# About 40 steps of a hand-ordered two-layer attention and expert kernel take other places in their engines' order

## The reference

```
x = x + attn1(ln(x))        # scores against 1601 memory tokens of the sequence, / 16, masked, softmax, readout
x = x + experts(ln(x))      # 8 experts (width 256), top 2 of the router: sum of w * (silu(h Wg) * (h Wu)) Wd
x = x + attn3(ln(x))        # q = h Wq; scores against the same 1601 tokens; only the 54 largest of a row stay; softmax; readout; Wo
x = x + ffn4(x)             # inputs rounded to 8 bits, weights to -1, 0, 1; w1 (256 to 1024), exact gelu, rounding, w2 (1024 to 256)
```

## Time and profile before

| | us |
|---|---|
| median of three runs | 501.22 |
| runs | 501.73, 499.03, 501.22 |
| the profiled execution | 500.69 |
| its span | 498.6 |
| outside the span | 2.1 |

### The profile page before, as it was taken

How to read it: one execution, slowest core, us unless ns; L and a number is a source line. 1 busy time by engine, 2 the same in 40 slices (tenths; PEclk the granted TensorE clock), 3 DMA queues, 4 the chain that set the end, 5 groups by cost and what they waited for, 6 DMA issues and landing times. The chain is left out here.

```text
span 498.6 us, 7119 instructions
## 1 busy us (share of the span) xinstructions
PE 418.6 (84%) x2445; PEld 342.0 (69%) x2452; DVE 381.3 (76%) x833; ACT 181.2 (36%) x264; POOL 92.5 (19%) x72
## 2 busy tenths in 40 slices
...
GB/s 248 350 238 216 157 140 227 133 97 163 175 132 107 149 170 128 136 176 139 169 189 78 152 140 116 176 143 152 102 23 11 133 5 128 0 111 3 11 0 11
DMA packets 60330, 63.96 MB, mean 128 GB/s; under 512 B 3964, under 2 KB 60040, under 8 KB 60296
## 3 DMA queue, kind: packets, MB, share of 16 engines
...
## 5 line engine op out<-in xcount | busy, mean ns | idle before, releaser
L482 POOL TENSOR_TENSOR gu_lo<-gu_stage,gu_hi 128x1024 fp32r<-128x1024 f32 x32 | 76.1, 2383 | 153.5 <-ACT gu_hi L547 153.5
L783 PE MATMUL O<-wd_ring,hid 128*128 128x256 f32 x256 | 62.8, 381 | 4.7 <-DVE x_res L968 4.5
L538 ACT ACTIVATE pT<-T 128x512 f32<-128x512 f32 x64 | 31.6, 513 | 80.0 <-PE T L721 69.4
L1017 DVE MAX8 cand_h<-fold 128x8 f32<-128x801 f32 x56 | 55.2, 985 | 0.3
L783 PEld LDWEIGHTS O<-wd_ring,hid 128*128 128x128 f32 x256 | 45.5, 189 | 12.4 <-DVE x_res L968 6.4
L739 PE MATMUL O<-pT,v_ring 128*128 128x128 f32 (+1 forms) x416 | 52.6, 287 | 0.3 <-ACT pT L538 0.3
L707 PE MATMUL S<-k_ring,xT 128*128 128x400 f32 (+2 forms) x128 | 49.4, 533 | 3.6 <-DVE mx1c L896 2.8
L739 PEld LDWEIGHTS O<-pT,v_ring 128*128 128x128 f32 (+1 forms) x416 | 51.1, 203 | 1.4 <-issue 1.1
L735 PE MATMUL O<-v_ring,pT 128*128 128x256 f32 (+1 forms) x208 | 48.1, 379 | 0.7 <-ACT pT L538 0.7
L1029 DVE MATCH_REPLACE8 fold<-cand_h,fold 128x801 f32<-128x801 f32 x48 | 46.9, 977 | 0.0
L554 ACT ACTIVATE hid<-G 128x512 f32<-128x512 f32 x32 | 19.1, 597 | 70.6 <-PE G L628 70.5
...
## 6 DMA issues: line engine op xcount, KB each, us to landing
...
```

Source lines behind the costliest of these rows:

```text
L482: pool.tensor_tensor(gu_lo[:, i % NG, :, :], gu_stage[:, i % NGS, :, :], gu_hi[:, i % NG, :, :].bitcast(F32), ALU.subtract).then_inc(lo_do ...
L538: act.activation(pT[0:r, i % NPT, :, :].rearrange("p a s -> p (a s)")[:, 0:w], t_bank(("pT", *key))[0:r, 0:w], ACT.Copy).then_inc(pTe_done, 1)
L783: mm = pe.matmul(o_bank(step)[:, 0:D], hid[:, j % NHID, f, i * P:(i + 1) * P], wd_ring[:, j % NWD, f, :], start=f == 0, stop=f == F // P - 1)
L1017: dve.max(cand_h[:, t % 2, 8 * r:8 * r + 8], fold[:, t % 2, 0:HALF]).then_inc(maxH_done, 1)
```

## The change

Only `ORDER` is written anew. The set of steps, their instructions, the tiles and the rings are the same. What is derived from the text follows: counts, the alternation of banks (two pairs of neighbours in class T, and one in class O, change places) and the order of SyncE's loads, where gate-up weights (0,0) now go ahead of k(1,0,0) and k(1,0,1), (0,2) ahead of k(1,1,1), and five pairs of wd and gu neighbours are swapped. The line breaks fall elsewhere, so most lines of the text differ; counted by the steps that no longer stand in the same sequence on their engine, TensorE has 53, ScalarE 31, VectorE 90 and GpSimd 1 (many of these are one swap of neighbours each). The lines on which the first steps stand, and those that hold the moves in later stretches:

```diff
--- before
+++ after
...
 ORDER = """
-stats.1.0 wrs aggr.1.0 stats.1.1 var.1.0 rstd.1.0 norm.1.0 aggr.1.1 xT.1.0 var.1.1 rstd.1.1 xTe.1.0 norm.1.1 mask.0
-s1.0.0 xT.1.1 s1e.0.0 s1.1.0 mask.1 s1.0.1 s1e.1.0 hi.0.0 hi.0.1 lo.0.0 xTe.1.1 s1.1.1 s1e.0.1 s1.0.2 s1e.1.1 s1.1.2
-s1e.0.2 s1.0.3 s1e.1.2 s1e.0.3 max1.0 exp1.0 pT.1.0.0 s1.1.3 pTe.1.0.0 pT.1.0.1 s1e.1.3 pT.1.0.2 pTe.1.0.1 pvm.1.0.0
-max1.1 pTe.1.0.2 exp1.1 r1.0 pT.1.0.3 pT.1.1.0 pTe.1.0.3 pT.1.1.1 pvm.1.0.1 pvm.1.0.2 pTe.1.1.0 wload.1 coef_e
-mask.2 pvm.1.0.3 pvm.1.1.0 x1.0 pTe.1.1.1 pvm.1.1.1 pT.1.1.2 pT.1.1.3 pTe.1.1.2 pTe.1.1.3 pvm.1.1.2 pvm.1.1.3 s1.2.0
-x1.1 stats.2.0 s1.2.1 aggr.2.0 var.2.0 s1e.2.0 rstd.2.0 lo.0.1 s1.2.2 norm.2.0 s1e.2.1 s1.2.3 s1e.2.2 xT.2.0 s1.3.0
...
-upd.0.1.1 wqb.1 hi.0.4 U.0.3 silu.0.3 lo.0.4 down.0.2.0 down.0.2.1 hi.0.5 G.0.4 exp1.3 mul.0.3 lo.0.5 upd.0.2.0
-upd.0.2.1 U.0.4 down.0.3.0 wload.2 silu.0.4 down.0.3.1 pT.1.2.0 hi.0.6 mul.0.4 G.0.5 upd.0.3.0 lo.0.6 upd.0.3.1
...
-hi.1.0 mul.0.7 upd.0.6.0 hi.1.1 upd.0.6.1 down.0.7.0 pTe.1.2.0 down.0.7.1 pTe.1.2.1 upd.0.7.0 pT.1.2.2 pT.1.2.3
...
-upd.1.5.0 merge.0 mul.1.6 lo.2.0 down.1.5.1 silu.1.7 U.1.7 upd.1.5.1 thr.0 exp3.0 down.1.6.0 mul.1.7 down.1.6.1
...
-upd.2.0.1 down.2.1.0 hi.2.4 xmx.0 xinv.0 maxH.2.6 down.2.1.1 lo.2.4 mul.2.2 G.2.3 xmul.0 xdeq.0 maxL.2.3 U.2.3
...
-upd.3.0.1 va4.3 q4.2 maxH.4.3 down.3.1.1 rs4.3 lo.3.4 upd.3.1.0 U.3.3 upd.3.1.1 hi.3.5 q4e.2 xnorm.3 up.2.0 xabs.3
...
-upd.3.7.0 upd.3.7.1 stats.3.3 merge.4 aggr.3.3 thr.4 var.3.3 pairH.5 exp3.4 rstd.3.3 maxL.5.0 maxH.5.0 norm.3.3
...
-gdeq.6 gmul.6 repH.7.4 gq.6 maxH.7.5 h4T.6 h4e.6 repH.7.5 dn.6 maxH.7.6 merge.7 thr.7 fin.6 cut.7.0 store.6 cut.7.1
...
-store.7
+mask.0 stats.1.0 aggr.1.0 stats.1.1 var.1.0 rstd.1.0 hi.0.0 norm.1.0 aggr.1.1 xT.1.0 var.1.1 rstd.1.1 xTe.1.0 lo.0.0
+norm.1.1 xT.1.1 s1.0.0 s1.1.0 s1e.0.0 s1.0.1 s1e.1.0 hi.0.1 wrs mask.1 s1.1.1 s1e.0.1 s1.0.2 s1e.1.1 s1.1.2 s1e.0.2
+s1.0.3 s1e.1.2 s1e.0.3 max1.0 exp1.0 xTe.1.1 pT.1.0.0 s1.1.3 pTe.1.0.0 pT.1.0.1 s1e.1.3 pT.1.0.2 pTe.1.0.1 pvm.1.0.0
+max1.1 pTe.1.0.2 exp1.1 r1.0 pT.1.0.3 pvm.1.0.1 pTe.1.0.3 pT.1.1.0 pT.1.1.1 pvm.1.0.2 pTe.1.1.0 coef_e pT.1.1.2
+pvm.1.0.3 pTe.1.1.1 pvm.1.1.0 mask.2 x1.0 pvm.1.1.1 pTe.1.1.2 pT.1.1.3 pvm.1.1.2 pTe.1.1.3 pvm.1.1.3 s1.2.0 x1.1
+stats.2.0 s1.2.1 aggr.2.0 var.2.0 s1e.2.0 rstd.2.0 lo.0.1 s1.2.2 norm.2.0 s1e.2.1 xT.2.0 s1.2.3 s1e.2.2 xTe.2.0
...
+down.0.0.1 upd.0.0.0 G.0.2 upd.0.0.1 wqa.1 U.0.2 silu.0.2 down.0.1.0 down.0.1.1 upd.0.1.0 wqs.1 G.0.3 upd.0.1.1
+mul.0.2 wqb.1 U.0.3 silu.0.3 hi.0.4 down.0.2.0 lo.0.4 down.0.2.1 hi.0.5 mul.0.3 wload.2 G.0.4 exp1.3 lo.0.5
...
+hi.1.0 upd.0.6.0 mul.0.7 hi.1.1 upd.0.6.1 down.0.7.0 pTe.1.2.0 down.0.7.1 pTe.1.2.1 upd.0.7.0 pvm.1.2.0 upd.0.7.1
...
+upd.1.4.0 repH.0.5 down.1.5.0 silu.1.6 maxH.0.6 U.1.6 upd.1.4.1 upd.1.5.0 down.1.5.1 pairH.1 hi.2.0 G.1.7 merge.0
...
+xnorm.0 xabs.0 U.2.2 upd.2.0.0 silu.2.2 upd.2.0.1 xmx.0 xdeq.0 xinv.0 maxH.2.6 down.2.1.0 repL.2.2 down.2.1.1 hi.2.4
...
+xq.2 ag4.3 mul.3.2 q4.2 va4.3 G.3.3 upd.3.0.1 lo.3.4 maxH.4.3 upd.3.1.0 down.3.1.1 q4e.2 hi.3.5 U.3.3 rs4.3
...
+exp3.4 rstd.3.3 norm.3.3 maxH.5.0 maxL.5.0 cut.4.0 repL.5.0 pT.3.4.0 pT.3.4.1 pTe.3.4.0 repH.5.0 pTe.3.4.1 pvm.3.4.0
...
+repH.7.3 gelu.6.1 gabs.6 maxH.7.4 gmx.6 ginv.6 gmul.6 gdeq.6 gq.6 repH.7.4 h4T.6 maxH.7.5 h4e.6 repH.7.5 dn.6
...
```

More of the change, by code:

```diff
@@ L72 @@
[L72 to L81, removed]
@@ L87 @@
[L87 to L96, removed]
@@ L102 @@
[L102 to L116, removed]
```

119 lines of the change are left out of this document (77 added, 42 removed).

## The result

The changed kernel takes 501.83 us (median of 16 runs, 498.84 to 504.38); the kernel before, over 16 runs beside it, 499.70 (498.54 to 501.73). The ratio is 1.0039, 95% interval 1.0022 to 1.0057: slower by 0.4%. The interval leaves out 1, so the loss is real, and it is smaller than the 0.5% that the prediction takes for no change.

The account below looks back on a forecast made before the run. TensorE was taken to bound 47 to 374 us and VectorE 374 to 471 us. The terms summed to +0.45 us, giving 501.1 by the profiled execution and 501.7 by the median; forecast 501.3 us, range 498.0 to 504.6.

Parts of the forecast that it names:

- (a): Start: lo.0.0 may take the port from norm.1.1 and delay the first score product; +0.6 us, bounds -0.5 to +1.7.
- (b): First attention: moved steps fill three TensorE gaps of 0.60, 0.67 and 1.77 us; -1.7 us, bounds -1.7 to 0.
- (c): 72 to 90 us: w2's issue ahead of exp1.3 delays silu.0.4 and G.0.5; +2.4 us, bounds +0.4 to +4.4.
- (d): 90 to 320 us: small swaps shorten x_res waits and others, some steps perhaps meet an lo; sum -0.95 us.
- (e): 320 to 350 us: gap before G.3.0 filled, but q4.2 waits for xnorm.2 beside lo.3.4; +0.3 us, bounds -0.6 to +0.8.
- (f): VectorE stretch: idle before norm.3.3, +0.6 us; small gaps filled in the tail, -0.8 us.
- Rival 2: Port lock between lo steps and VectorE falls against the new order at four places: about 505 us; chance 0.15.
- My last sign of being wrong: Small shifts re-deal lo ties where nothing was moved, each worth 2.0 us, two exceeding the whole sum.
- The busy times: All engines' busy times stay within 1% in the changed profile, but for the stretched VectorE steps.
- Rival 1: Faster: gaps are filled and the price at 75 to 90 us isn't paid, about 498.5 us; 0.27 with what lies beyond.
- Rival 4: ScalarE's chain at 72 to 90 us is worth double: +2.0 us more, about 503.3 us; chance 0.10.
- Rival 3: Nothing to be seen: moves lie where the moved engine isn't last, 501.2 us; chance 0.48 together with the forecast.

Follow-up runs that it names:

- after: The changed kernel with the whole new order, against the kernel before: 501.83 us, ratio 1.0039.
- exp_ahead: The changed kernel with one swap on ScalarE, exp1.3 ahead of w2's transfer issue (wload.2): 501.36 us, ratio to the kernel before 1.0034.
- q4_behind: The changed kernel with TensorE issuing q4.2 behind down.3.1.1, no longer ahead of G.3.3: 502.06 us, ratio to the kernel before 1.0047.
- Experiment 4: The changed kernel with rs4.3 ahead of lo.3.4 on GpSimd, gu(3,6) and wd(3,4) swapping back too: 499.08 us, ratio to the kernel before 1.0002.
- Experiment 8: The changed kernel with rs4.3 ahead of lo.3.4, hi.3.7 ahead of silu.3.5, norm.3.3 behind maxH.5.0: 496.86 us, ratio to the kernel before 0.9963.
- experiments 1 and 2: New order up to U.2.7, the order before behind it: 498.47 us, ratio 0.9971; the reverse: 503.10 us, 1.0072; both against the kernel before.

## Why the prediction was right, and which of its terms were not

The forecast, no change that can be told, and the range held: 501.83 us against 501.3. That the two times lie so close is luck twice over. The forecast of a time stood on a median of 501.22 from three runs of the kernel before; over 16 runs it is 499.70. As a change, the sum said +0.45 us and +2.1 was measured, in the profiled pair +3.4. And the sum came out small by errors that cancelled, as its terms show.

- **(a) Start, +0.6 as the half of -0.5 and +1.7.** In the profile the meeting took place: +1.55. It took place in four of the seven profiles with this start: the mechanism was right, and the even odds fit as far as seven show. I had it hang on the weights; the landing of x decided.
- **(b) Three gaps, -1.7.** Measured -2.13, beyond its bound of -1.7: 0.79 and 0.91 at the first two, for 0.60 and 0.67, and 0.44 at the third.
- **(c) w2's issue ahead of the exponential, +2.4.** Measured +2.41 at G.0.5, by a chain that agrees link for link (silu.0.4 ends at 86.6, with the 0.58 us by which the new order is ahead there 87.2, for 87.3); 0.78 us come back by wqs.2. Undone, it gave 1.74 us in the trace. The wait of 1.17 us for lo.0.4 I hadn't named: I had seen that lo.0.4 would come at 77 us, not that G.0.4 needed it. It adds nothing, since U.0.4's wait falls by as much; the shift at U.0.4, +0.65 from s1.3.0, is mul.0.2 ahead of wqb.1, which I had at +0.67. The load is again 1.28 us with the next step 0.01 to 0.02 us behind it, so the drain of 1.38 us that the Trainium skill gives for a switch ("ScalarE: Activation LUTs", "What ACT_TABLE_LOAD costs") does not stand between them here either.
- **(d) 90 to 320 us, -0.95.** Measured -1.00 from wqs.2 up to U.2.7, and this agreement is luck as well. rt2.1 gave 0.74 and U.2.0 net 0.40, near their terms. The swaps of 254 to 285 us gave some 2.0, not 0.5. Against them stand +1.04 at U.1.6, which I hadn't named: upd.1.4.0 is late there by pairL.1, blocked 1.07 us longer under lo.1.6 and lo.1.7, and by mul.1.5 (0.67 us) in front of it, shares that no experiment takes apart. There are also some +0.4 from pairH.1, and +0.9 at 253 to 259 us, most of it since upd.2.1.1 now stands behind xnorm.1, which lo.2.5 blocks. I had put +0.5 on xdeq.0 there, which isn't blocked (0.16 us). pairH.1 took 1.50 us in after, 2.94 and 3.00 in exp_ahead and q4_behind.
- **(e) 320 to 350 us, +0.3 with bounds of -0.6 and +0.8: the step that failed.** Its gains were 1.76 us, 0.76 at G.3.0 for the 1.0 I gave it and 0.97 at U.3.2, from mul.3.1 ahead of repH.4.2, for which I had nothing; its price was +4.33. I had both pieces, lo.3.4 beside xnorm.2 and q4.2 ahead of G.3.3, and netted them by guess, instead of following the chain: 2.0 us of block, passed on in full to xq.2 and to q4.2, and TensorE idle for 3.1 us with nothing to hide it. I also left out the low clock behind the idle stretch: 1.3 us on G.3.3 and 0.3 on down.3.1.1. Experiment 4 takes the block away, and the wait's 2 us and the low clock go with it.
- **(f) VectorE stretch: norm.3.3 +0.6, measured +0.67; the tail -0.8, measured -1.90.**
- **Not foreseen at all:** lo.3.7 on gdeq.3, +2.0 us, from the move of hi.3.7 behind silu.3.6, and pairL.1 under (d). At gdeq.3 I had read VectorE's, TensorE's and GpSimd's moves, not when GpSimd's input would be ready. Experiment 8 takes this one away.

Rival 2, that the port lock falls against the new order, named the right mechanism. Of its four places two fell so, the start at about my price and (e) far above it; pairH.1 did in some executions, xdeq.0 did not. It did not carry the median beyond 0.5%, since (d), (e)'s gains and the tail gave 4.7 us. My last sign of being wrong, that ties are drawn anew where I priced none, came true at pairL.1 and gdeq.3. The busy times did not all stay within 1% either: GpSimd's rose by 2.9%, since an lo that is blocked is longer too (lo.1.7 took 3.14 us for 2.39). Rival 1 was half true: the gaps were worth what it said, but (c)'s price was paid. Rival 4 was wrong, nothing added to (c) downstream. Rival 3's premise, that the moves lie where nothing is last, is refuted by experiments 1 and 2, which have opposite signs.
